# Taking the stage between two layers apart into single steps of the next sequence's first-layer pass

## What is computed

```python
# layer 0, attention: 16 heads, query and key 96 wide (64 of them rotated), value 32 wide
nq  = rms(x @ w_cq);  q = [nq @ w_dq_nope, rope(nq @ w_dq_rope)]
ckv = rms(x @ w_ckv); k1 = [ckv @ w_dk_nope, rope(x @ w_krope / 16)]; v1 = ckv @ w_dv
idx = sort(top_k(x @ w_imp, 64)); ks, vs = x[idx] @ w_selk, x[idx] @ w_selv   # 64 chosen tokens
kw, vw = x @ w_wink, x @ w_winv
out = g0 * attn(q, k1, v1, causal) + g1 * attn(q, ks, vs) + g2 * attn(q, kw, vw, causal)
x = x + out @ w_proj                                    # g = softmax(mean(x @ w_gate))
# layer 0, second part: 5 steps of a spiking neuron over a feed-forward product
y = relu(x @ W_fc.T) ** 2 @ W_proj.T                    # 1024 hidden units
x = x + sum(spikes of y over 5 steps) / 5
# layer 1, attention: 16 heads of width 16, causal; second part: one product
x = x + attn(rope(q), rope(k), v) @ W_o.T
x = x + x @ weight.T
```

## Time and profile before

| | |
|---|---|
| median of 3 runs | 3427.34 us (3424.78 to 3427.54) |
| the profiled execution | 3425.91 us, of which the span of its instructions is 3424.2 us |
| PE busy | 3139.8 us (92%), mean granted clock 0.955 of full speed |
| DVE, ACT, POOL busy | 1956.8 us (57%), 1550.6 us (45%), 924.3 us (27%) |
| one sequence, start to start | 419.7 us: about 242 first-layer pass, 8 projection, 82 stage between the layers, 88 second-layer pass |

### The profile page before, as it was taken

The page is one execution under the profiler, slowest core; times in us unless marked ns, Lnnn a source line. Parts: engine busy times, 40 slices in busy tenths (PEclk is TensorE's granted clock), DMA queues, the critical chain, the costliest instruction groups (busy, mean ns, idle before and its releaser), DMA issues. The chain is left out here.

```text
span 3424.2 us, 58117 instructions
## 1 busy us (share of the span) xinstructions
PE 3139.8 (92%) x20368; PEld 2280.3 (67%) x20368; DVE 1956.8 (57%) x6865; ACT 1550.6 (45%) x3410; POOL 924.3 (27%) x1828
## 2 busy tenths in 40 slices
PE   4999799997999979999899988999889998899978
PEld 3776667765677756776567765677656776567755
DVE  4664556646566465664756646566365664665535
ACT  1554345534454344553445535445354552545524
POOL 0222322222222222222222332222322323222222
PEclk7999999999999999999999999999999999999989
DMA  2000000000000000000000000000000000000000
GB/s 96 20 20 13 0 13 20 20 13 1 19 13 20 13 1 20 20 14 13 1 19 20 20 7 1 20 20 20 7 1 25 16 17 7 1 26 20 1 1 7
DMA packets 30063, 51.78 MB, mean 15 GB/s; under 512 B 3408, under 2 KB 12368, under 8 KB 29520
## 3 DMA queue, kind: packets, MB, share of 16 engines
q1 hardware_dynamic: 29776, 48.07, 4.3%
HBM read 43.86 MB, written 4.19 MB: 14 GB/s over the span
## 5 line engine op out<-in xcount | busy, mean ns | idle before, releaser
L1519 ACT ACTIVATE PR<-work 128x512 f32<-128x512 f32 (+1 forms) x1088 | 641.2, 599 | 564.7 <-PE work L899 470.8
L1162 DVE CUSTOM_DVE_ANT_0 work<-work,KEEPB 128x384 f32<-128x384 f32 (+3 forms) x1536 | 666.7, 482 | 67.8 <-PE work L860 66.8
L1647 POOL TENSOR_SCALAR_AFFINE_SELECT PR<-PR 128x256 f32<-128x256 f32 (+1 forms) x960 | 348.9, 367 | 913.7 <-ACT PR L1519 909.5
L860 PE MATMUL work<-BIG 96*128 96x448 f32 (+9 forms) x1664 | 436.2, 356 | 38.5 <-DVE NMX L1162 14.2
L1144 DVE TENSOR_TENSOR BIG<-work,BIG 96x512 fp32r<-96x512 f32 (+1 forms) x448 | 280.3, 628 | 322.7 <-ACT BIG L1413 321.6
L1637 POOL TENSOR_TENSOR TOK<-AB 128x256 f32<-128x256 f32 (+1 forms) x320 | 216.1, 675 | 840.1 <-DVE AB L1114 835.4
L897 PE MATMUL work<-BIG 99*128 99x512 f32 (+4 forms) x1152 | 404.7, 351 | 0.3
L941 PE MATMUL outs<-PR,ONES 128*32 128x512 f32 (+4 forms) x2304 | 404.4, 458 | 0.0
L860 PEld LDWEIGHTS work<-BIG 96*128 96x128 f32 (+1 forms) x1664 | 269.7, 196 | 182.0 <-issue 91.6
L1113 DVE TENSOR_TENSOR AB<-work,COS 128x256 f32<-128x256 f32 (+2 forms) x352 | 148.3, 421 | 424.4 <-PE work L816 343.4
L898 PE MATMUL work<-BIG 96*128 96x512 f32 (+4 forms) x1152 | 382.5, 332 | 0.0
(11 more groups left out here) (161 smaller groups left out, 5145.8 us busy)
## 6 DMA issues: line engine op xcount, KB each, us to landing
WKW<-w_kw_dram SPq DMA_DIRECT2D x64, 256.0 KB, 2.7
WSEL<-w_sel_dram SPq DMA_DIRECT2D x64, 256.0 KB, 2.9
X<-x_dram SPq DMA_DIRECT2D x8, 512.0 KB, 3.9
out_dram<-X SPq DMA_DIRECT2D x8, 512.0 KB, 2.9
WFC<-w_fc_dram SPq DMA_DIRECT2D x1, 1024.0 KB, 9.8
WFP<-w_ffp_dram SPq DMA_DIRECT2D x1, 1024.0 KB, 11.9
WQKV<-w_qkv_dram SPq DMA_DIRECT2D x1, 768.0 KB, 13.2
WQ<-w_q_dram SPq DMA_DIRECT2D x1, 576.0 KB, 7.3
```

The lines of the kernel that those rows point to most:

```text
L860: last = mm(ps[:, col:col + n], q, k, start=(i_mm == 0), stop=(i_mm == len(u["mm"]) - 1))
L1162: last = v.tensor_tensor_reduce(ps[:, lo:hi], ps[:, lo:hi], KEEPB[:, T - (hi - lo):T], -1.0, -NEG, ALU.add, ALU.min, dst)
L1519: a.activation(PR[0:rows, j % NP, :], ps[0:rows, :], ACT.Exp).then_inc(exp_ready, 1)
L1647: gp.affine_select(blocks, blocks, [[0, len(cols)], [1, P]], ALU.is_ge, 0.0, base=0, channel_multiplier=-1).then_inc(exp_masked, 1)
```

## The change

The list of passes becomes `PASSES`: first-layer pass 0, first-layer pass 1, second-layer pass 0, first-layer pass 2, second-layer pass 1, and so on, and at the end second-layer passes 6 and 7. So the second layer of a sequence follows one first-layer pass later than before. The stage between the layers of sequence n is cut into single steps with numbers of their own (`MID`, `HEADS`) and sorted into the list of first-layer pass n+1 (for the last sequence into second-layer passes 6 and 7). The whole prologue of sequence n+2 (`PRO`) goes into the same first-layer pass, the ranking too, which leaves the second-layer pass. The projection (`PROJ`) moves to the start of the second-layer pass that follows. The spike product `y` no longer has banks of its own: it holds one of the five work banks from its first product until the spikes are counted (`hold`). One of the four copies per stack transpose goes from ACT to DVE (`heads_out`). Some buffers move: `R2` is a tensor of its own, both stacks lie in `PR`, `X0` is gone, and x is loaded twice, once into `HN0` for the norm and once into `X1` for the residual. All arithmetic is the same in kind and amount.

```diff
+PASSES = [(0, 0)] + [z for n in range(1, B) for z in ((0, n), (1, n - 1))] + [(1, B - 1)]
...
+PRO = [("pro", 0, 62.0), ("pro", 1, 63.5), ("pro_pe", 0, 75.0), ("pro_act", 2, 75.1), ("pro_pe", 1, 77.0),
+       ("pro_act", 3, 77.1), ("pro", 3, 78.0), ("pro_pe", 6, 79.0), ("pro_act", 4, 79.1), ("pro_pe", 2, 81.0),
...
+MID = [[("ln", 1, 0, 1.0), ("ln", 1, 1, 1.6), ("hT", 1, 0, 2.5), ("hT", 1, 1, 3.0)]
+       + [("fc", 0, f, 5.0 + 3 * f) for f in range(4)]
+       + [("y", 0, tt, 17.5 + 4 * tt) for tt in range(2)] + [("spikes", 0, 23.5)]
+       + [("fc", 1, f, 26.0 + 3 * f) for f in range(4)]
+       + [("y", 1, tt, 39.0 + 4 * tt) for tt in range(2)] + [("spikes", 1, 45.0)]
...
+HEADS = [[("clear", 0, 94.5), ("clear", 1, 98.6), ("stack", 0, 95.5), ("stack", 1, 99.0), ("heads", 0, 98.2), ("heads", 1, 100.2),
+          ("stack", 2, 100.3), ("heads", 2, 101.85), ("stack", 3, 102.1), ("heads", 3, 103.5), ("v", 0, 104.0), ("v", 1, 104.5)],
...
     if layer == 0:
...
+        if s:
+            add(MID[0], s - 1)
+            add(HEADS[0], s - 1)
+        if s < B - 1:
+            add(PRO, s + 1)
...
-MID_STEPS = [("fc", 0, 0), ("fc", 0, 1), ("fc", 0, 2), ("fc", 0, 3), ("y", 0, 0), ("y", 0, 1), ("pro_pe", 0), ("pro", 2),
...
+    def hold(self, name):
+
+        self.use(name)
+        self.held.add(self.of[name][0])
...
+            elif what == "y" and x[3] == 0:
+                work.hold(("y", n, x[2]))
+            elif what == "spikes":
+                work.held.discard(work.of["y", n, x[2]][0])
...
-            for s in range(B):
-                attention(0, s)
...
+            for z in PASSES:
+                attention(*z)
...
+                for threshold in THRESHOLDS[1:-1]:
+                    then(v.scalar_tensor_tensor(total, ps[:, :], threshold, total, ALU.is_ge, ALU.add))
+                ins = v.scalar_tensor_tensor(total, ps[:, :], THRESHOLDS[-1], total, ALU.is_ge, ALU.add)
+                read_work(ins, use)
```

More of the change, by code:

```diff
@@ L148 @@
 AFTER = [dict(pv=2.67, tr=1.82, sum=0.75, group=1.98, piece=-2.58, gap=0.66, piece_tr=2.36, max=4.9, max_gap=0.31,
[L149 to L158 removed]
+              mt=2.12, rows=-5.38),
@@ L180, in attention_steps @@
                     at.append((t1 + 0.1 + o["sum"], ("sum", p)))
-                if group and layer == 0 and p == NPAIR - 1:
-                    at.append((t1 + o["group"] - 0.01, ("projection",)))
                 if group:
@@ L242 @@
+    return [x for _, x in sorted(at, key=lambda x: x[0])]
+STEPS = {z: attention_steps(*z) for z in PASSES}
 class Banks:
@@ L299, in attention @@
     def attention(layer, s):
-        for x in steps(layer, s):
-            if x[0] == "mt" and layer == 0:
+        for x in STEPS[layer, s]:
+            what, n = x[0:2]
+            if what == "mt" and layer == 0:
                 for h in range(2):
                     work.use((s, 0) + x + (h,))
-            elif x[0] in ("unit", "max", "mt", "out_tr", "group"):
-                work.use((s, layer) + x, {"unit": 0, "mt": 2}.get(x[0], 1))
-            elif x[0] in ("piece", "piece_tr"):
-                piece(NPAIR * s + x[1], x[2], x[0])
-            elif x[0] == "projection":
-                for i in range(2):
-                    work.use((s, "proj", i))
-            elif x[0] == "pro_pe":
-                prologue(s + 1, x[1])
-            elif x[0] == "tail_pe":
-                tail(s - 1, x[1])
+            elif what in ("unit", "max", "mt", "out_tr", "group"):
+                work.use((s, layer) + x, {"unit": 0, "mt": 2}.get(what, 1))
+            elif what in ("piece", "piece_tr"):
+                piece(n, x[2], what)
+            elif what == "pro_pe":
+                prologue(n, x[2])
+            elif what == "tail_pe":
+                tail(n, x[2])
             elif x == ("add_group", 0):
@@ new lines, in second_products @@
+            def second_products(n, i, tt):
+                use = ("y", n, i)
+                ps = take(use, W)[0] if tt == 0 else WB[work.of[use][0]]
+                for f in range(NF):
+                    if tt == 0 and f % 2 == 0:
+                        pe.wait_ge(squared, NF * n + NF // 2 * i + f // 2 + 1)
+                    units = R2[:, f // 2, (f % 2) * 256 + tt * P:(f % 2) * 256 + (tt + 1) * P]
+                    last = mm(ps[:, tt * C:(tt + 1) * C], units, WFP[:, f, :], start=(f == 0), stop=(f == NF - 1))
+                if tt:
+                    last.then_inc(work_full[work.of[use][0]], 1)
@@ L951, in attention @@
             def attention(layer, s):
-                for x in steps(layer, s):
+                for x in STEPS[layer, s]:
                     if x[0] == "piece":
-                        piece(NPAIR * s + x[1], x[2])
-                    elif x[0] == "projection":
-                        for i in range(2):
-                            proj_banks.append(take((s, "proj", i), W))
-                        for g in range(NG - 1):
-                            was_read(pe, work, work_read, (s, 0, "group", g))
-                            for i in range(2):
-                                add_group(proj_banks[i][0], i, g, WP)
+                        piece(x[1], x[2])
```

790 lines of the change are left out of this document (400 added, 390 removed).

## The result

The changed kernel takes 3484.5 us (median of four runs, 3478.89 to 3490.49) against 3427.4 us before: 1.0168 times as long, 95% interval 1.0150 to 1.0186. The forecast was 3411 us with a range up to 3475, so the result lies outside the range, on the other side.

The account below looks back on a forecast made before the run. PE, busy 3139.8 of 3424.2 us, bounds the kernel. Per steady sequence +10.3 + 3.0 - 2.7 - 11.1 + 2.3 = 1.8 us won; with first pass and last stage 16 us off, 3411 us, range 3335 to 3475.

Parts of the forecast that it names:

- Chains that go: Stage between the layers: PE's waits for normalised rows (8.9 us) and ACT's copy (1.4) vanish, 10.3 us won per stage.
- Start of the second-layer pass: First 24 us of the second-layer pass: ranking leaves, projection comes, idle falls from 5.5 to 2.5 us, a gain of 3.0.
- The stack transposes: End of the first-layer pass: four transposes in a row, 9.9 us idle against 7.2 before, a loss of 2.7 per sequence.
- DVE's inserted work: First-layer pass: PE waits on banks and results while DVE does the added steps, 11.1 us lost per sequence, bounds 5 and 18.
- POOL's steps, costed at nothing: Prologue in the first-layer pass: POOL's squares, 1.0 us each, hide behind the 2.67 units that `pv` lags its exponentials.
- The first pass and the last stage: Ends of the run: 3 us lost in the first pass, 6 won in the last stage (16 idle after, 22.1 before).
- The clock: Slow stretches of the stage: 5.0 us go, 2.7 set for new ones, a gain of 2.3 us per sequence.
- The clock pays it back: Rival: spike and ranking waits each end in a 2.0 us slow stretch, products after the stacks run slow; 3455 us, chance 0.11.
- The row that the prediction held against it: Evidence against the clock paying back: second-layer pass 2 keeps a clock of 1.00 with 5.5 us idle in 24.
- Slack hides it: Rival: DVE catches up in its idle 43%, inserted work costs 5 us, stacks no more than now; 3349 us, chance 0.30.
- the ring decides: Rival: work banks around the spike counts and prologue's squares hold PE, inserted work costs 18 us; 3459 us, chance 0.17.
- a first-layer clock under 0.95: Sign that the forecast is wrong: the granted clock of a first-layer pass falls from 0.98 to below 0.95.

Follow-up runs that it names:

- one place later: Changed kernel with PE's prefix sums of the mask moved behind one step of values' products instead of ahead of it: 3440.8 us, ratio 1.0039.
- the wait put into the kernel before: Kernel before the change, with PE's prefix sums of the mask one unit and its products earlier in the second-layer pass: 3448.0 us, ratio 1.0051.
- the combined kernels: Changed kernel with ranking steps early, or prefix sums and gathering later plus tail steps later; both with spike counts cut and POOL's attention sum earlier: 3361.1 and 3355.9 us.
- The run with POOL's steps moved: Changed kernel with the fourth rotation's sum and the power of the next sequence's norms moved behind two causal masks on POOL: 3488.8 us, ratio 1.0180.
- the counts cut: Changed kernel with each spike count split into two steps one unit apart, comparisons, then residual and variances: 3427.4 us, ratio 1.0003.
- four edits of this kind: Changed kernel with ranking steps early, spike counts cut, prefix sums and gathering later, and stacks built ahead of the previous copies: 3318.5 us, ratio 0.9680.

## Why the prediction was wrong, step by step

**Chains that go** (+10.3). Right: waits for normalised rows remain at the tail alone, and the copy's wait is gone.

**Start of the second-layer pass** (5.5 to 2.5 us idle). Right. The first 24 us:

```profile
1135.30:1159.30 24.00, 21.73 (x110) 0.93 0.00 0
```

2.3 us idle. But the clock is 0.93 where the earlier trace rows had 1.00.

**The stack transposes** (4.6, 6.1 and 5.2 us apart; 9.9 idle). Nearly right: 4.5, 6.9 and 5.4, idle 8.7, with the wait for the sum at 4.05 against 4.1. PE's timeline, start and length:

```profile
1110.75 1.97 PE L1069 MATMUL work<-ID,PR 128*128 128x128 f32 x16
...
1115.29 1.97 PE L1069 MATMUL work<-ID,PR 128*128 128x128 f32 x16 [1.96 <-POOL PR L1770]
...
1121.30 1.11 PE L1010 MATMUL work<-ID,NRM 128*128 128x128 f32 x4 [4.05 <-POOL NRM L1728]
1122.21 2.96 PE L1069 MATMUL work<-ID,PR 128*128 128x128 f32 x16
...
1127.64 3.60 PE L1069 MATMUL work<-ID,PR 128*128 128x128 f32 x16 [2.46 <-POOL PR L1770]
```

**DVE's inserted work** (11.1). Right in kind and a little high. The bank of the first count 2.1 (forecast 2.2), the ranking 2.4 (2.2), the second count 2.0 (2.9), the wait of 1.2 behind the first count all but absent; with the short ones of 0.1 to 0.7 us about 9 us.

**POOL's steps, costed at nothing.** Wrong: 4.6 us of waits for masks. I checked the squares, and not the rotation sums and the power of the prologue, which are also inserted ahead of masks. POOL works in its order, so it stands at the sum until DVE has rotated and then at the power until DVE has the variances, and the masks queue behind. POOL's timeline:

```profile
1449.72 1.27 POOL L1752 TENSOR_TENSOR R<-HN 128x512 f32<-128x512 f32 x1 [4.48 <-DVE HN L1177]
1451.65 1.02 POOL L1688 TENSOR_TENSOR YP<-VAR,MHALF 128x4 f32<-128x4 f32 x1 [0.66 <-DVE VAR L1165]
1452.63 1.02 POOL L1717 TENSOR_SCALAR_AFFINE_SELECT PR<-PR 128x128 f32<-128x128 f32 x3
```

Taken together the idle terms came out as forecast, and partly by luck: this miss of 4.6 stands against the two terms set too high, by 1.2 and about 2. The sum had 0.5 us more idle time over the whole run (seven times 0.5 lost, 3 lost in the first pass, 6 won in the last stage); the page shows 3.5 more. The first pass and the last stage were not measured apart.

**The clock** (+2.3 per sequence). This is the step that failed. The gain was taken to be 5.0 for the slow stretches of the stage, less 2.7 for new ones, and the 2.7 is the term that was mis-sized. Four of the new waits that the first-layer pass now holds have slow stretches of 13.6, 6.8, 3.4 and 3.4 us (ranking, mask, the two counts), and 25.5 us of them lie on work: 12.7 us lost, ten more than was set. The ranking's 2.4 us of waiting takes another 6.4, the mask's 3.0 another 2.9, each count's 2.0 another 1.7. With 12.7 in place of 2.7 the term is -7.7; the profile shows -7.4 (51.7 by 7), 9.7 less than +2.3 and 68 us in all. The forecast for the span was 3408; with these 68, the 9.4 left over and 3.0 us more idle time than forecast it is 3488, and the span is 3488.8. Two experiments with the wait alone show that it is the cause: one place later, 7 us less wait and 44 less time; the wait put into the kernel before, 22 us more. They show it for the ranking wait; taking the mask wait away gave nothing back, and its share is read from the trace alone.

**The rivals.** 'The clock pays it back' named the mechanism, with a chance of 0.11 and 3455 us: it took 2.0 us for each slow stretch from the earlier trace rows and had none at the masks. The row that the prediction held against it, a clock of 1.00 with 5.5 us idle in 24, is right for second-layer pass 2 and not for the kernel. The same 24 us of passes 1, 3 and 4:

```profile
831.00:855.00 24.00, 19.32 (x109) 0.93 0.00 1
1670.40:1694.40 24.00, 19.74 (x103) 0.86 0.00 1
2090.40:2114.40 24.00, 19.63 (x105) 0.86 0.00 1
```

Only passes 0 and 2 stay at 1.00; in the other five, 1 and 3 to 6, the clock is 0.86 or 0.93, with waits of at most 1.7 us. So the trace of the kernel before held evidence for this rival; the pass that was read is one of the two without it. 'Slack hides it' and 'the ring decides' fall: the inserted work cost about 9 us, against 5 and 18. The forecast had named a first-layer clock under 0.95 as a sign of being wrong; it is 0.94.

The Trainium skill, TensorE: Matmul & The Clock Gate, section on HAM oscillation, has a recurring wait pay the slow start every time. The changed kernel agrees: the ranking wait has its 13.6 us slow in each of the seven passes. The other runs agree only in part, with five of seven passes for the wait put into the kernel before and three to five of six for the mask wait in the combined kernels. The same page, in the section "A second HAM failure mode: psum-queue depth-cycling", says that small pauses of PE between groups of products, as it cycles through its banks, can make the clock swing too. The run with POOL's steps moved shows small pauses before such a fall: pauses that add up to 1.7 us in 8, and then 6.8 us at 0.50. But the longest of them, 1.24 us, is a wait for row maxima from DVE, so whether cycling through the banks has a part in it isn't shown.

**What stays open.** The same 3.0 us wait has a slow stretch in three or four of six passes of two kernels and in all of a third, and the same 2.4 us wait in one execution (the counts cut) has 3.4, 10.2, 13.6 or 20 us. In the kernel before, PE waits 2.4 us for the first stack in the middle of every one of its seven steady stages, and the clock stays up each time:

```profile
1212.00:1214.00 2.00, 0.12 (x1) 1.00 0.00 0
1214.00:1216.00 2.00, 2.00 (x18) 1.00 0.04 8
```

The runs show what such a wait costs on average in these places, not which one will cost it.

## What to carry to other kernels

In this kernel, with PE over 90% busy, a new wait of 2 to 3 us in the dense pass cost on average 1.6 to 3.7 times its length. Count such a wait at more than its length, and look first for a step that can be moved ahead of it: one step moved by one place was worth 44 us here. Moving chains beside dense work is worth it only when the consumers come late enough: the change by itself lost 57 us, and with four edits of this kind it wins 109. Before one row is held against a rival, read the same place in every repetition: the row used here was one of two in seven. After a change compare idle time and busy time apart; equal instruction counts with more busy time point at the clock before anything else.

## What the runs showed of the hardware

A granted clock of 0.50 lasted 13.6 to 20 us at one wait of 2.4 us, with PE busy throughout behind it (10.00 of 10 us in a window of the longer one); in the steady sequences the slow stretches last between 3.4 and 20 us, and one of 37.5 us stands at the start of the changed kernel. The mixture of work alone doesn't explain them, since the same products run at 1.00 when the wait is gone (16 products of 64 columns: 3.51 and 1.89 us). And identical waits of 2.97 us in one execution are followed by the lower level or not, pass by pass. In the changed kernel, where every steady sequence takes the same 430 us, nearly every wait has the same stretch in each of them.
